# First attention of a four-layer model: the triangular inverses of the chunks as 64x64 tiles in two quadrants of TensorE, all sixteen token tiles in one pass

## What is computed

```python
C = 64                                   # tokens of a chunk
Kb = K * bta; Vb = V * bta
A = jnp.einsum('bnihd,bnjhd->bnij', Kb, K)           # per chunk, summed over the heads
T0 = jnp.eye(C) - jnp.tril(A, -1)
def body(i, T):
    row = jax.lax.dynamic_slice_in_dim(T, i, 1, axis=2)[:, :, 0]
    acc = jnp.einsum('bnj,bnjc->bnc', row, T)
    new_row = jnp.where(col < i, row + acc, row)
    return jax.lax.dynamic_update_slice_in_dim(T, new_row[:, :, None, :], i, axis=2)
T = jax.lax.fori_loop(1, C, body, T0)
W = jnp.einsum('bnij,bnjhd->bnihd', T, Kb)
U = jnp.einsum('bnij,bnjhd->bnihd', T, Vb)
```

## Time and profile before

| | us |
|---|---|
| median of 3 runs | 3692.62 (3683.25 to 3702.91) |
| the profiled execution | 3694.0 |
| its span, first to last instruction | 3692.3 |
| of it, phase of the inverse | 148.2 to 275.1 |
| of it, phase of W and U | 275.3 to 309.1 |

### The profile page before, as it was taken

The page is one execution under the profiler, slowest core; times in us unless marked ns, Lnnn a source line. Parts: engine busy times, 40 slices in busy tenths (PEclk is TensorE's granted clock), DMA queues, the critical chain, the costliest instruction groups (busy, mean ns, idle before and its releaser), DMA issues. The chain is left out here.

```text
span 3692.3 us, 51962 instructions
## 1 busy us (share of the span) xinstructions
PE 2948.2 (80%) x17269; PEld 1736.6 (47%) x17301; DVE 1994.7 (54%) x4847; ACT 1544.3 (42%) x4324; POOL 698.2 (19%) x753
## 2 busy tenths in 40 slices
PE   6475795763899998667976998989978868959993
PEld 3471463231555555334643554435533445636662
DVE  6546575362678876485834663236622556842223
ACT  4211494231677776343133652215621227813331
POOL 3200102011211220001202661025600112301113
PEclk9596898876999999888987999999999979959997
DMA  1000002001000000000000000000000000051112
GB/s 64 1 1 0 14 2 75 0 14 49 1 2 2 2 2 21 36 1 12 2 15 30 1 1 32 0 30 1 1 32 0 18 20 2 2 211 33 31 34 76
DMA packets 34786, 80.40 MB, mean 22 GB/s; under 512 B 8577, under 2 KB 23570, under 8 KB 30450
## 3 DMA queue, kind: packets, MB, share of 16 engines
q1 hardware_dynamic: 28738, 63.30, 4.7%
q0 software_dynamic: 4368, 11.93, 1.2%
q10 hardware_dynamic: 1440, 2.12, 0.2%
HBM read 63.31 MB, written 14.02 MB: 21 GB/s over the span
## 5 line engine op out<-in xcount | busy, mean ns | idle before, releaser
L2288 ACT ACTIVATE scores<-scores,min 128x128 f32<-128x128 f32 (+7 forms) x256 | 198.5, 775 | 86.0 <-DVE min L2271 81.7
L2269 DVE TENSOR_SCALAR zero_marks<-psum 128x128 f32<-128x128 f32 (+7 forms) x256 | 192.2, 751 | 66.6 <-PE psum L2201 64.4
L2271 DVE CUSTOM_DVE_ANT_0 scores<-psum,zero_marks 128x128 f32<-128x128 f32 (+7 forms) x256 | 194.0, 758 | 29.9 <-issue 0.9
L2208 PE MATMUL psum<-ident,scores 128*128 128x128 f32 x1152 | 172.8, 277 | 16.7 <-ACT probsT L2305 13.7
L2305 ACT ACTIVATE probsT<-psum 128x128 f32<-128x128 f32 (+7 forms) x256 | 163.2, 638 | 31.6 <-PE psum L2208 30.6
L3499 PE MATMUL psum<-Hn,W 128*128 128x512 f32 x384 | 168.7, 602 | 9.0 <-PEq L394 9.0
L1494 ACT ACTIVATE XT<-psum,b_of_tile 128x128 f32<-128x128 f32 x312 | 89.1, 369 | 171.4 <-PE psum L1404 171.4
L1396 PE MATMUL psum<-W,x_gatheredT 128*128 x312 | 149.2, 602 | 1.7 <-DVE x_gatheredT L1451 1.7
L2208 PEld LDWEIGHTS psum<-ident,scores 128*128 128x128 f32 x1152 | 123.2, 141 | 56.3 <-issue 30.9
L2198 PE MATMUL psum<-XT,Q_heads 64*128 64x512 f32 x256 | 143.7, 641 | 0.0
L1412 PE MATMUL psum<-W,XT 128*128 x624 | 141.2, 379 | 1.0 <-ACT XT L1494 1.0
(11 more groups left out here) (616 smaller groups left out, 7091.9 us busy)
## 6 DMA issues: line engine op xcount, KB each, us to landing
W<-in_L3f_W SPq DMA_DIRECT2D x16, 1024.0 KB, 22.6
L3f_y_rows<-y SPq DMA_DIRECT2D x39, 128.0 KB, 1.7
L0f_rows<-Xtok SPq DMA_DIRECT2D x2, 2048.0 KB, 8.0
W<-in_L0f_W SPq DMA_DIRECT2D x3, 1152.0 KB
Wqkv<-in_L2f_Wqkv SPq DMA_DIRECT2D x2, 1536.0 KB, 8.3
W<-in_L2f_W SPq DMA_DIRECT2D x2, 1536.0 KB
XT<-in_xT SPq DMA_DIRECT2D x1, 2048.0 KB, 7.9
Xtok<-in_xtok SPq DMA_DIRECT2D x1, 2048.0 KB, 13.1
```

Of the source, the lines that this page charges most:

```text
L2208: ins = pe.transpose(turned[:, kt * P:(kt + 1) * P], Sc[:, i % ROT, kt * P:(kt + 1) * P], K.ident[:])
L2269: dve.tensor_scalar(zero[:, i % 2, 0:n], sc(i)[:, 0:n], 0.0, -NEG, ALU.is_equal, ALU.mult)
L2271: dve.tensor_tensor_reduce(Sc[:, i % ROT, 0:n], sc(i)[:, 0:n], zero[:, i % 2, 0:n], 1.0, -NEG, ALU.add, ALU.min, low[:, i % ROT:i % ROT + ...
L2288: act.activation(p, p, ACT.Exp, bias=low[:, i % ROT:i % ROT + 1], scale=-1.0, accum_out=sums[:, u % 2, h:h + 1]).then_inc(s["exp_done"], 1)
```

## The change

`GT` becomes 8 and a tile's matrix is kept as `[128, 64]`: partitions 0 to 63 hold the first chunk of a token tile, partitions 64 to 127 the second. Eight tiles x 64 columns again fill one bank, so the two groups now hold all sixteen tiles and there is one pass instead of two rounds.

- Each matmul on 128x128 becomes two on 64x64, `for own in halves`: weights and moving operand on partitions 0:64 with output on partitions 0:64, then the same for 64:128. These are the upper left and the lower right quadrant of the array. Both write the same PSUM bank. In the products of A the contraction is still over 128 partitions, so there the two matmuls are two column halves of the array (128x64).
- The products are pipelined by one tile: the transposes of tile n + 1 stand ahead of the matmuls of tile n.
- GpSimd cuts the masks and the identity to `[128, 64]` at the start of the phase (four copies), and VectorE waits for them.
- VectorE's drains become waits on semaphores, and four of the five `E_T` are cut after `M_T` and `M` are made; the number and size of its instructions per group is as before.
- `T_transposed` is `[128, 16, 64]`, and the matmul of W and U becomes two, 64 weights against 512 columns each, in the two quadrants.

```diff
@@ -2817,101 +2817,115 @@
                             pool.tensor_tensor(v, v, inner(nr[:, t, 0:L0H], D // L0H), ALU.mult)
-            TT = sbuf(q_life, nc, "T_transposed", [P, NT, P])
+            TT = sbuf(q_life, nc, "T_transposed", [P, NT, CH])
             with ExitStack() as inn:
-                GT = 4
+                GT = NT // 2
+                LAST = LEVELS - 1
                 kT = sbuf(inn, nc, "kT", [P, 2, 2 * DC * P])
-                E = sbuf(inn, nc, "E_T", [P, 2, LEVELS - 1, GT, P])
-                M, MT, X = (sbuf(inn, nc, n, [P, 2, GT, P]) for n in ("M", "M_T", "X"))
-                four = lambda ap: middle(ap, GT)
+                E = sbuf(inn, nc, "E_T", [P, 2, LAST, GT, CH])
+                M, MT, X = (sbuf(inn, nc, n, [P, 2, GT, CH]) for n in ("M", "M_T", "X"))
+                cmask = sbuf(inn, nc, "masks_in_chunk", [P, LEVELS + 2, CH])
+                halves = (slice(0, CH), slice(CH, P))
+                all_of = lambda i: middle(cmask[:, i, :], GT)
+                unit = all_of(LEVELS + 1)
                 part = lambda u, i: K.bank[2 + 3 * u + i]
-                bank4 = lambda u, i: part(u, i)[:].rearrange("p (t k) -> p t k", t=GT)
-                names = "k_turned k_out a_done0 a_done1 m_ready0 m_ready1 x_done0 x_done1 x_out0 x_out1 y_done0 y_done1"
+                tiles_of = lambda u, i: part(u, i)[:].rearrange("p (t k) -> p t k", t=GT)
+                names = "k_turned k_out masks_cut a_done0 a_done1 cut0 cut1 m_ready0 m_ready1 x_done0 x_done1 x_out0 x_out1 y_done0 y_done1 doubled"
                 with phase(nc, K.sems, names) as (block, s):
                     a_done, m_ready, x_done = (s["a_done0"], s["a_done1"]), (s["m_ready0"], s["m_ready1"]), (s["x_done0"], s["x_done1"])
-                    x_out, y_done = (s["x_out0"], s["x_out1"]), (s["y_done0"], s["y_done1"])
-                    ROUNDS = NT // (2 * GT)
+                    x_out, y_done, cut = (s["x_out0"], s["x_out1"]), (s["y_done0"], s["y_done1"]), (s["cut0"], s["cut1"])
+                    @block.gpsimd
+                    def _(pool):
+                        for own in halves:
+                            pool.tensor_copy(cmask[own, 0:LEVELS + 1, :], masks[own, :, own]).then_inc(s["masks_cut"], 1)
+                            pool.tensor_copy(cmask[own, LEVELS + 1, :], K.ident[own, own]).then_inc(s["masks_cut"], 1)
                     @block.tensor
                     def _(pe):
...
+                        def a_of(u, i):
+                            t = u * GT + i
+                            if t >= 2:
+                                pe.wait_ge(s["k_out"], t - 1)
+                            for c in range(DC):
+                                pe.transpose(K.bank[t % 2][:, c * P:(c + 1) * P], QK[:, t, D + c * P:D + (c + 1) * P], K.ident[:])
+                                ins = pe.transpose(K.bank[t % 2][:, (2 + c) * P:(3 + c) * P], KV[:, t, c * P:(c + 1) * P], K.ident[:])
+                            ins.then_inc(s["k_turned"], 1)
+                        def a_products(u, i):
+                            t = u * GT + i
+                            pe.wait_ge(s["k_out"], t + 1)
+                            k_, kb = (lambda c: kT[:, t % 2, c * P:(c + 1) * P]), (lambda c: kT[:, t % 2, (2 + c) * P:(3 + c) * P])
+                            for held, moved, to in ((k_, kb, 1), (kb, k_, 2)):
+                                for c in range(DC):
+                                    for own in halves:
+                                        ins = pe.matmul(part(u, to)[own, i * CH:(i + 1) * CH], held(c)[:, own], moved(c)[:, own], start=(c == 0), stop=(c == DC - 1), skip_group_check=True)
+                            ins.then_inc(a_done[u], 1)
+                        def chunk_products(u, to, held, moved):
                             for i in range(GT):
...
+                                for own in halves:
+                                    ins = pe.matmul(part(u, to)[own, i * CH:(i + 1) * CH], held[own, i, :], moved[own, i, :], start=True, stop=True, skip_group_check=True)
+                            return ins
+                        order = [(u, i) for u in range(2) for i in range(GT)]
+                        for n, (u, i) in enumerate(order):
+                            a_of(u, i)
+                            if n >= 1:
+                                a_products(*order[n - 1])
+                        a_products(*order[-1])
+                        for lv in range(1, LEVELS):
                             for u in range(2):
...
+                                pe.wait_ge(m_ready[u], lv)
+                                chunk_products(u, 0, E[:, u, lv - 1], M[:, u]).then_inc(x_done[u], 1)
+                            for u in range(2):
+                                pe.wait_ge(x_out[u], lv)
+                                chunk_products(u, 1, MT[:, u], X[:, u])
+                                chunk_products(u, 2, X[:, u], MT[:, u]).then_inc(y_done[u], 1)
                     @block.scalar
                     def _(act):
...
+                        for t in range(NT):
+                            act.wait_ge(s["k_turned"], t + 1)
+                            if t >= 2:
+                                act.wait_ge(a_done[(t - 2) // GT], (t - 2) % GT + 1)
+                            act.activation(kT[:, t % 2, :], K.bank[t % 2][:], ACT.Copy).then_inc(s["k_out"], 1)
+                        for lv in range(1, LEVELS):
+                            for u in range(2):
+                                act.wait_ge(x_done[u], lv)
+                                if lv >= 2:
+                                    act.wait_ge(y_done[u], lv - 1)
+                                act.activation(X[:, u], tiles_of(u, 0), ACT.Copy).then_inc(x_out[u], 1)
                     @block.vector
                     def _(dve):
...
+                        dve.wait_ge(s["masks_cut"], 4)
+                        for u in range(2):
+                            dve.wait_ge(a_done[u], GT)
+                            dve.tensor_tensor(MT[:, u], tiles_of(u, 1), all_of(0), ALU.mult)
+                            dve.tensor_tensor(M[:, u], tiles_of(u, 2), all_of(LEVELS), ALU.mult).then_inc(cut[u], 1)
+                            dve.tensor_tensor(E[:, u, 0], tiles_of(u, 1), all_of(1), ALU.mult)
+                            dve.wait_ge(cut[u], 1)
+                            dve.tensor_tensor(MT[:, u], unit, MT[:, u], ALU.subtract)
+                            dve.tensor_tensor(M[:, u], unit, M[:, u], ALU.subtract)
+                            for lv in range(2, LEVELS):
+                                ins = dve.tensor_tensor(E[:, u, lv - 1], tiles_of(u, 1), all_of(lv), ALU.mult)
+                            ins.then_inc(m_ready[u], 1)
+                        for lv in range(1, LEVELS):
                             for u in range(2):
...
+                                dve.wait_ge(y_done[u], lv)
+                                dve.wait_ge(m_ready[u], lv)
+                                dve.tensor_tensor(M[:, u], M[:, u], tiles_of(u, 1), ALU.subtract)
+                                dve.tensor_tensor(MT[:, u], MT[:, u], tiles_of(u, 2), ALU.subtract).then_inc(m_ready[u], 1)
+                        for u in range(2):
+                            dve.tensor_scalar(X[:, u], unit, -2.0, None, ALU.mult).then_inc(s["doubled"], 1)
+                        for u in range(2):
+                            dve.wait_ge(m_ready[u], LEVELS)
+                            dve.wait_ge(s["doubled"], u + 1)
+                            dve.scalar_tensor_tensor(out=TT[:, u * GT:(u + 1) * GT, :], in0=MT[:, u], scalar=3.0, in1=X[:, u], op0=ALU.mult, op1=ALU.add)
             sums = sbuf(q_life, nc, "chunk_sums", [P, 2 * DC, NCH])
@@ -2938,7 +2952,9 @@
                     def products(t):
                         if t >= 2:
                             pe.wait_ge(s["wu_out"], t - 1)
-                        pe.matmul(K.bank[t % 2][:], TT[:, t, :], KV[:, t, :], start=True, stop=True).then_inc(s["wu_done"], 1)
+                        for own in (slice(0, CH), slice(CH, P)):
+                            ins = pe.matmul(K.bank[t % 2][own, :], TT[own, t, :], KV[own, t, :], start=True, stop=True, skip_group_check=True)
+                        ins.then_inc(s["wu_done"], 1)
                     products(0)
                     products(1)
                     pe.wait_ge(s["step"], 5)
```

More of the change, by code:

```diff
@@ L2837, in _ @@
                     @block.tensor
                     def _(pe):
-                        def a_of(r, u):
-                            for i in range(GT):
-                                t = (2 * r + u) * GT + i
-                                if t >= 2:
-                                    pe.wait_ge(s["k_out"], t - 1)
-                                for c in range(DC):
-                                    pe.transpose(K.bank[t % 2][:, c * P:(c + 1) * P], QK[:, t, D + c * P:D + (c + 1) * P], K.ident[:])
```

(11 more changed lines are left out.)

48 lines of the change are left out of this document (removed).

## The result

The changed kernel takes 3630.61 us in the median of 4 runs (3624.47 to 3631.03), the kernel before 3687.93 in 4 runs taken beside them and earlier (3679.88 to 3702.91). The ratio is 0.9836, with a 95% interval of 0.9801 to 0.9871. The profiled execution took 3631.03 us with a span of 3629.2, against 3694.0 and 3692.3 before: 63 us less, where the prediction had 66.

The account below looks back on a forecast made before the run. TensorE waits for ScalarE's copy in the products, VectorE alone works in the masks, TensorE almost bounds the levels. 18.9 + 5.7 + 34.2 = 58.8 us for 126.9, 66 less with the allowance: 3627 us, range 3612 to 3667.

Parts of the forecast that it names:

- the inverse: Whole phase of the inverse: 58.8 us instead of 126.9, 68 us less, or 66 with 2 us taken off.
- W and U: Matmul of W and U as two quadrant matmuls: 0 us if they run as pairs, +13.7 us in single file.
- Products: Products of sixteen tiles: 18.9 us instead of 47.4; 1.89 us a tile at 1.2 GHz, 1.07 after the clock rises at 3.7 us.
- ScalarE's copy: In the products: 0.60 us and some 0.2 of hand-over, covered by neighbouring tiles' matmuls and transposes, which take 1.07.
- Masks: VectorE's mask instructions: group 0's 5.6 us hidden behind tiles 8 to 15, group 1's exposed at 5.7 us.
- Levels and end: Five levels run once and the end: 34.2 us, as round 2 took, with pairs at full overlap, 0.056 us each.
- allowance of 2: In the levels: 2 us taken off the gain for dearer pairs, 4 ns over 480 pass pairs in five levels.
- (1): Levels, W and U: quadrants writing one PSUM bank go one after the other; 3667 us, 3674 with the products; chance 0.10.
- (2): Levels: quadrants overlap but each record has a floor of issue, 40 to 50 ns; 3639 to 3648 us; chance 0.14.
- (3): Clock stays at 1.2 GHz where two of four quadrants work; 3651 to 3675 us, in products only 3638; chance 0.07.
- (4): Levels, W and U: single file and low clock feed each other, a level 21.3 us; 3754 us, slower than before; chance 0.03.
- (5): The change doesn't do what it says; dismissed, as instruction order shows one pass with five levels; no chance of its own.

## Why the prediction held, and where its terms were off

**In total.** 3627 was forecast and 3630.61 came, inside the range. By parts, against the profiled execution: the inverse 58.8 + 2 predicted, 63.2 measured; W and U 0 predicted, -2.0 measured (from its first matmul to the copy of the sums: 244.94 - 211.78 = 33.2 us, after 310.61 - 275.44 = 35.2 before). That makes 65.7 us where 66 were forecast. Errors of +2.4 and -2.0 cancelled, so the close sum is partly luck. By the medians of the runs the gain is 3687.93 - 3630.61 = 57 us, less than by the profiled pair; the runs of the kernel before spread over 23 us. The span fell by 63.1, 2.6 less than the two phases; the two traces differ by that elsewhere, which is within the spread of the runs.

**Products, 18.9 predicted, 21.9 measured.** This is the term that was mis-sized. Two steps of it failed. First, a tile takes 1.21 us and not 1.07 at the high clock, 2.10 and not 1.89 at the low one. I had taken 0.09 us for each of the two changes of shape, from one place that goes from whole to narrow matmuls. The step across that change is 0.09 longer here too, but the narrow run and the step behind the way back are longer as well, and per tile the two changes cost 1.21 - 0.44 - 0.45 = 0.32 us instead of 0.18. Over thirteen tiles at the high clock that is 1.8 us. Second, the clock rose 5.8 us into the phase and not after 3.7. The 3.7 came from a single rise; in the traces of changed kernels whose products start at 1.2 GHz, rises came 2.9 to 5.9 us in. A single rise gives no better than that. The later rise is what is left to account for the remaining 1.2 us or so.

**ScalarE's copy** is hidden, as said. It stands at 156.78 beside the products of the tile before, and no PE row has a wait on it. The kernel without the pipeline shows what else hung on that in a phase that starts at 1.2 GHz: the clock.

**Masks, 5.7 predicted, 5.6 measured**, group 0's hidden.

**Levels and end, 34.2 plus an allowance of 2 predicted, 35.8 measured.** The pair costs 0.058 us and not 0.056, and a level took 6.27 for 6.11: 0.8 us over five levels. The clock's low stretch lasted 6.8 us (174.6 to 181.4), where round 2 of the kernel before had 3.4; that is the likely source of the other 0.8. The allowance, meant for dearer pairs alone, happened to cover both.

**W and U.** No cost for the pairs, as said. Left out were two things: a pair is 0.05 us cheaper than the whole matmul, and the phase's stretch of low clock has a length of its own in each trace.

**The rivals.** (1) Single file did not happen: both quadrants write one bank and run at 0.058 us a pair. The Trainium skill, TensorEngine Tiling (Array Packing), Gotcha 1: PSUM Pressure, says that different row tiles cannot access one bank at the same time. By these 0.058 us a pair the trace of the level's products does not agree, for two quadrants that write different partitions of the bank. (2) A floor of issue did not show: 32 records in 0.93 us is 29 ns each, under the 40 ns that I had as the densest. (3) The clock rose during the transposes and products, and again in the levels; a clock that stays low in the products only, which stood at 3638, is not what the trace shows, as the window from 154.1 to 170.1 has 1.00. (4) Of the mechanism of the slow case, single file and low clock feeding each other, one direction is real: undoing the pairing kept a clock that had fallen at 1.2 GHz through all levels, at 16.08 us a level where the rival had 21.3, and cost 48 of the 57 us that were gained. But single file did not pull down a clock that was up (9.31 us a level), and its seams still overlapped. I gave this rival 0.03; it was one order of two loops away. (5) The change did what it says.

## What to carry to other kernels

Two quadrants on the diagonal do twice the small matmuls in the same time, if the program's order alternates between them at least every two matmuls; written quadrant by quadrant, most of the overlap is lost and the clock may not come back. A wait of some tenths of a microsecond per tile should be priced at both clocks: where the tiles followed on 32 us of idleness it kept the clock at 1.2 GHz (2.86 us a tile, 45 us in all), and in a round that followed on busy levels it did not (2.28 us a tile). Before counting narrow matmuls as half of whole ones, add the change of shape in both directions, measured over a whole round trip: it ate 0.32 of the 0.44 us that they saved per tile here.

## What the runs showed of the hardware that I had not expected

- TensorE starts records of a later matmul in an idle quadrant ahead of up to three records of earlier ones: the six seam records start within 0.17 us (190.28 to 190.45), where in single file five steps of 0.058 would lie between the first and the last, 0.29.
- With one quadrant at work at a time the granted clock stayed where it was, down for the 78 us of five levels and up for the 28 us of three, in both cases with TensorE busy almost throughout; each was seen in one run. With pairs, or pairs with single matmuls between them, it rose 1.9 to 5.7 us after they began.
- A set of 48 records in two quadrants, 32 to 16, takes the time of the 32: 1.87 us, 0.058 each.
